# Opening of a cross-attention block: the query weights split by column groups, four token blocks turned in a row, small vectors on another queue

## The reference, cut to what matters

```python
x = x + _L0_xattn_ref(_layernorm(x, axis=-1), ctx_1024, ctx_1024, mask, W_q, b_q, W_k, b_k, W_v, b_v, W_o, b_o)

def _L0_xattn_ref(q, k, v, mask, ...):
    Q = split_heads(q @ W_q + b_q)      # 16 heads of 32
    K = split_heads(k @ W_k + b_k)
    V = split_heads(v @ W_v + b_v)
    scores = jnp.einsum('bhqd,bhkd->bhqk', Q, K) / math.sqrt(D_K)
    ...
```

## Time and profile before

| what | us |
|---|---|
| median of three runs | 741.67 |
| the profiled execution | 741.27 |
| its span, first to last instruction | 739.5 |
| PE busy | 709.2 |
| DVE busy | 406.5 |
| ACT busy | 326.5 |
| POOL busy | 202.7 |

### The profile page before, as it was taken

How to read it: one execution, slowest core, us unless ns; L and a number is a source line. 1 busy time by engine, 2 the same in 40 slices (tenths; PEclk the granted TensorE clock), 3 DMA queues, 4 the chain that set the end, 5 groups by cost and what they waited for, 6 DMA issues and landing times.

```text
span 739.5 us, 18487 instructions
## 1 busy us (share of the span) xinstructions
PE 709.2 (96%) x7369; PEld 575.9 (78%) x7384; DVE 406.5 (55%) x1089; ACT 326.5 (44%) x700; POOL 202.7 (27%) x160
## 2 busy tenths in 40 slices
PE   4999999999999999999999999999998999999976
PEld 1788888888888888888888888877776767766743
DVE  4833323323665345345343323349478888887886
ACT  3425456455344344344344344455224524433434
POOL 2610001000987647647530000001122122113110
PEclk9999999999999999999999999999999999999999
DMA  7242333332132231231121121626001011101201
GB/s 256 93 175 61 120 122 107 128 121 89 36 122 84 89 118 35 89 117 36 32 64 32 32 64 33 228 60 242 1 1 30 1 42 43 43 1 43 43 1 44
DMA packets 46632, 56.83 MB, mean 77 GB/s; under 512 B 15088, under 2 KB 35824, under 8 KB 45328
## 3 DMA queue, kind: packets, MB, share of 16 engines
q1 hardware_dynamic: 41840, 39.20, 17.3%
q0 software_dynamic: 3328, 16.78, 6.4%
q10 hardware_dynamic: 1440, 0.53, 0.3%
HBM read 51.19 MB, written 2.16 MB: 72 GB/s over the span
## 4 chain that ended last, share of the span: by engine, by line
PE 82%; DVE 10%; issue 4%; DMA 2%; ACT 1%; SPq 0%; DVEq 0%; POOL 0%; ACTq 0%
PE bank L231 66%; PE bank L437 4%; PE bank L595 3%; PE bank L451 3%; PE bank L428 3%; DVE s_sb L1388 2%; DMA stage<-in_w_xq 2%; PE bank L558 1%; DMA stage<-in_w_xo 1%; DVE X L1446 1%; DVE y_quant L1354 1%; DVE h_max L1395 1%; DVE h_sb L1372 0%; DVE y_sb L1363 0%; PE bank L459 0%
## 5 line engine op out<-in xcount | busy, mean ns | idle before, releaser
L231 PE MATMUL bank<-ctx_high,wk_high 128*128 128x258 f32 x512 | 147.4, 288 | 0.1
L231 PE MATMUL bank<-ctx_low,wk_high 128*128 128x258 f32 x512 | 144.6, 282 | 0.0
L231 PE MATMUL bank<-ctx_high,wk_low 128*128 128x258 f32 x512 | 144.1, 282 | 0.0
L231 PEld LDWEIGHTS bank<-ctx_high,wk_high 128*128 128x128 f32 x512 | 96.8, 189 | 13.7 <-issue 13.4
L231 PE MATMUL bank<-wv_high,ctx_high 128*128 128x512 f32 x256 | 105.9, 414 | 0.0
L791 ACT ACTIVATE vals<-bank 128x512 f32<-128x512 f32 x64 | 38.3, 598 | 144.2 <-PE bank L231 144.2
L231 PE MATMUL bank<-wv_low,ctx_high 128*128 128x512 f32 x256 | 101.2, 395 | 0.0
L231 PE MATMUL bank<-wv_high,ctx_low 128*128 128x512 f32 x256 | 100.9, 394 | 0.0
L231 PEld LDWEIGHTS bank<-ctx_low,wk_high 128*128 128x128 f32 x512 | 96.7, 189 | 0.0
L231 PEld LDWEIGHTS bank<-ctx_high,wk_low 128*128 128x128 f32 x512 | 96.5, 188 | 0.0
L781 ACT ACTIVATE kT<-bank,bxk 128x257 f32<-128x257 f32 x128 | 60.3, 473 | 56.5 <-PE bank L231 56.3
(11 more groups left out here) (217 smaller groups left out, 1359.0 us busy)
## 6 DMA issues: line engine op xcount, KB each, us to landing
raw<-in_ctx_t SPq DMA_DIRECT2D x32, 514.0 KB, 4.0
stage<-in_w POOLq DMA_DIRECT2D x16, 1024.0 KB, 5.9
X<-in_x SPq DMA_DIRECT2D x4, 512.0 KB, 4.2
v_last<-last_values SPq DMA_DIRECT2D x32, 64.0 KB
out<-X SPq DMA_DIRECT2D x8, 256.0 KB, 2.3
stage<-in_w_xv SPq DMA_DIRECT2D x1, 1024.0 KB, 8.1
stage<-in_w_xq SPq DMA_DIRECT2D x1, 1024.0 KB, 11.5
stage<-in_w_xk SPq DMA_DIRECT2D x1, 1024.0 KB, 5.7
```

The lines of the kernel that those rows point to most:

```text
L231: last = pe.matmul(to, left(i, c), right(j, c), start=(c == 0 and i + j == 0), stop=(c == C - 1 and i == 1))
```

## The change

- The query weights are split in four groups of 128 output columns, each over all four chunks: ACT makes the four high parts one after the other, DVE the four low parts. POOL's part in it is gone. Each of the first four query products waits for its own group (`wxq_low`, and `weights_low` for the fourth).
- Token blocks use three PSUM banks (0, 1, 2) instead of two, so `turn_x(t)` waits for `x_low(t - 3)`. `xn` still has two buffers.
- ACT copies all four first blocks before it touches the query weights. DVE measures blocks 2 and 3 before it scales block 0, and finishes the four `x_low` before the four low parts of the weights.
- PE turns blocks 2 and 3 after `project_last(0)` and does `project_last(1..3)` behind them; blocks 4 and 5 are turned after queries 1 (before: after queries 0), 6 and 7 after queries 2 (before: after queries 1). ACT follows: `keep_queries(0)`, `keep_queries(1)`, blocks 4 and 5, `keep_queries(2)`, blocks 6 and 7, W_v.
- The eight small transfers are issued by SP behind W_q instead of by ACT.

```diff
 # SP
             load_weight(1)
             load_weight(0)
+            for dst, src in small:
+                sp.dma_start(dst, src).then_inc(small_landed, 16)
             staged_ready(sp, 0)
 # PE
-                if t >= 2:
-                    pe.wait_ge(xT_low, t - 1)
+                if t >= 3:
+                    pe.wait_ge(xT_low, t - 2)
...
+                if half == 0:
+                    pe.wait_ge(*((wxq_low, g + 1) if g < C - 1 else (weights_low, 1)))
...
             project_last(0)
             turn_x(2)
-            project_last(1)
             turn_x(3)
-            project_last(2)
-            project_last(3)
-            pe.wait_ge(weights_low, 1)
-            pe.wait_ge(wxq_rest_low, 1)
-            for k in range(2):
-                project_queries(k)
-                turn_x(4 + 2 * k)
-                turn_x(5 + 2 * k)
+            for c in range(1, C):
+                project_last(c)
+            project_queries(0)
+            project_queries(1)
+            turn_x(4)
+            turn_x(5)
             project_queries(2)
+            turn_x(6)
+            turn_x(7)
 # ACT
-            for dst, src in small:
-                act.dma_start(dst, src).then_inc(small_landed, 16)
...
-            x_high(0)
-            x_high(1)
+            for t in range(C):
+                x_high(t)
             staged_ready(act, 0)
-            act.activation(wxq[0][:, 2:4, :], stage[0][:, 2:4, :], ACT.Copy).then_inc(wxq_rest_high, 1)
-            x_high(2)
-            act.activation(wxq[0][:, 0:2, :], stage[0][:, 0:2, :], ACT.Copy).then_inc(weights_high, 1)
-            x_high(3)
+            for g in range(C):
+                part = slice(g * P, (g + 1) * P)
+                act.activation(wxq[0][:, :, part], stage[0][:, :, part], ACT.Copy).then_inc(
+                    wxq_high if g < C - 1 else weights_high, 1)
...
-            for k in range(2):
-                keep_queries(k)
-                x_high(4 + 2 * k)
-                x_high(5 + 2 * k)
+            keep_queries(0)
+            keep_queries(1)
+            x_high(4)
+            x_high(5)
+            keep_queries(2)
+            x_high(6)
+            x_high(7)
             split_weight(1)
-            keep_queries(2)
             keep_queries(3)
 # POOL
-                if k == 2:
-                    pool.wait_ge(wxq_rest_high, 1)
-                    pool.tensor_tensor(wxq[1][:, 2:4, :], stage[0][:, 2:4, :], wxq[0][:, 2:4, :].bitcast(F32),
-                                       ALU.subtract).then_inc(wxq_rest_low, 1)
 # DVE
             measure_x(0)
+            measure_x(1)
             scale_x(0)
-            measure_x(1)
             scale_x(1)
+            scale_x(2)
             x_low(0)
-            scale_x(2)
-            x_low(1)
             scale_x(3)
-            x_low(2)
-            dve.wait_ge(weights_high, 1)
-            dve.tensor_tensor(wxq[1][:, 0:2, :], stage[0][:, 0:2, :], wxq[0][:, 0:2, :].bitcast(F32),
-                              ALU.subtract).then_inc(weights_low, 1)
-            x_low(3)
+            for t in range(1, C):
+                x_low(t)
+            for g in range(C):
+                part = slice(g * P, (g + 1) * P)
+                dve.wait_ge(*((wxq_high, g + 1) if g < C - 1 else (weights_high, 1)))
+                dve.tensor_tensor(wxq[1][:, :, part], stage[0][:, :, part], wxq[0][:, :, part].bitcast(F32),
+                                  ALU.subtract).then_inc(wxq_low if g < C - 1 else weights_low, 1)
```

More of the change, by code:

```diff
@@ L168, in build_block @@
         weights_high, weights_low = sem("weights_high"), sem("weights_low")
-        lastT_landed, wxq_rest_high, wxq_rest_low = sem("lastT_landed"), sem("wxq_rest_high"), sem("wxq_rest_low")
+        lastT_landed, wxq_high, wxq_low = sem("lastT_landed"), sem("wxq_high"), sem("wxq_low")
         placed_landed = {"v": sem("v_landed"), "g": sem("g_landed")}
@@ L270, in load_weight @@
                     sp.wait_ge(weights_low, n - 1)
-                    if n == 2:
-                        sp.wait_ge(wxq_rest_low, 1)
                     if n == 3:
@@ L356, in turn_x @@
                 pe.wait_ge(x_scaled, t + 1)
-                if t >= 2:
-                    pe.wait_ge(xT_low, t - 1)
+                if t >= 3:
+                    pe.wait_ge(xT_low, t - 2)
                 for c in range(C):
-                    last = pe.transpose(bank[t % 2][:, c * P:(c + 1) * P], xn[:, t % 2, c * P:(c + 1) * P], idf[:, :])
+                    last = pe.transpose(bank[t % 3][:, c * P:(c + 1) * P], xn[:, t % 2, c * P:(c + 1) * P], idf[:, :])
                 last.then_inc(x_turned, 1)
@@ L741, in x_high @@
                 act.wait_ge(x_turned, t + 1)
-                act.activation(xT[t // C][0][:, :, t % C * P:(t % C + 1) * P], bank[t % 2][:, :].rearrange("p (c n) -> p c n", c=C),
+                act.activation(xT[t // C][0][:, :, t % C * P:(t % C + 1) * P], bank[t % 3][:, :].rearrange("p (c n) -> p c n", c=C),
                                ACT.Copy).then_inc(xT_high, 1)
@@ L1153, in x_low @@
                 high, low = [part[:, :, t % C * P:(t % C + 1) * P] for part in xT[t // C]]
-                dve.tensor_tensor(low, bank[t % 2][:, :].rearrange("p (c n) -> p c n", c=C),
+                dve.tensor_tensor(low, bank[t % 3][:, :].rearrange("p (c n) -> p c n", c=C),
                                   high.bitcast(F32), ALU.subtract).then_inc(xT_low, 1)
```

## The result

Nine runs of the changed kernel gave a median of 739.59 us (738.44 to 741.62), nine of the kernel before beside them 742.32 us (741.31 to 743.54). The ratio is 0.9967, with a 95% interval of 0.9956 to 0.9978: by the ratio 2.45 us faster, and between 1.6 and 3.3 (the two medians alone differ by 2.73). The prediction was 740.0 us with a gain of 1.65 us, "same within 0.3%" at 0.67. The time lies in the range of 738.6 to 741.6; the gain is larger than forecast and on the far side of the 0.3% line, though its interval reaches back over it. The profiled execution lasted 739.59 us, and 739.6 was forecast for it.

What follows compares the result with a forecast made beforehand. TensorE's opening, up to the first key matmul, was taken to decide: 2.05 us gained at the queries less 0.4 given back makes 1.65, so 741.27 falls to 739.6, or 740.0 us on the median's footing; range 738.6 to 741.6.

Steps and rivals of the forecast that it cites:

- The bound: Loop from 43.60 to 464 us: TensorE works without a hole, so any opening shift passes undiminished to the end.
- K: Start of the first key matmul, ending the opening; 43.60 us before, forecast near 42.0.
- TensorE up to the queries: Opening: first transposes move from 8.28 to 8.75 us, then work without gaps; queries forecast to start at 17.1.
- S: Start of the first query matmul; 19.15 us before, forecast 17.1.
- the clock's share: Opening: the clock's rise puts the query start between 16.4 (splits then limit it) and 18.0; gains 2.3 to 0.7 us.
- the forecast's first condition: Opening: TensorE's clock rises 4.4 us after unbroken work begins, near 13.2 us.
- Weights and small vectors: Opening: weight splits don't decide the query start, and moving eight small transfers to SP has price 0.
- From S to the keys: First query to first key matmul: 24.9 us, with about 1.2 us waiting for the context behind POOL's addition.
- The term that was mis-sized: Gain at the start of the queries: forecast 2.05 us, of which 0.4 is given back before the keys.
- A: At the keys: context not late, TensorE alone decides; keys at 40.8, gain 2.8 us, 738.9 us; chance 0.17.
- B: Opening: small vectors hold SP, x blocks 4 to 7 issued 3.7 us later; gain 1.0, 740.7 us; chance 0.08.
- C: Opening: TensorE stays at 1.2 GHz, keys at 45.2; 1.6 us later, 743.3 us; chance 0.06.

Runs made afterwards that it cites:

- Experiment 5: Changed kernel with twenty unread identity transposes on TensorE ahead of block 0; 738.10 us, ratio 0.9940 to the kernel before.
- experiment 1: Changed kernel with GpSimd's bias addition put behind the second context split; 738.15 us, ratio 0.9937 to the kernel before.
- experiment 3: Changed kernel with blocks 4 and 5 turned after queries 0, 6 and 7 after queries 1; 741.91 us, ratio 0.9983 to the kernel before.
- experiment 6: Changed kernel with both the twenty early transposes and GpSimd's addition behind the second context split; 736.05 us, ratio 0.9923 to the kernel before.
- experiment 4: Changed kernel with the eight small transfers issued by ACT again; 739.48 us, ratio 0.9961 to the kernel before.
- Experiment 10: Changed kernel with project_last(1) between the turns of blocks 2 and 3; 740.11 us, ratio 0.9965 to the kernel before.
- experiment 2: Kernel before with GpSimd's bias addition put behind the second context split; 742.77 us, ratio 1.0002.
- again: Kernel before, unchanged, profiled once more in one execution; 743.38 us.
- experiment 9: Kernel before with ten identity transposes behind project_last(3), filling the gap before the queries; 741.92 us, ratio 1.0001.
- experiment 7: Kernel before with twenty identity transposes on TensorE ahead of block 0; 743.06 us, ratio 1.0007.
- experiment 8: Kernel before with only the low part of W_q's chunks 2 and 3 moved from GpSimd to VectorE; 741.98 us, ratio 0.9987.

## Why the prediction was right, and where it was off

**The bound.** From 43.60 us on a shift passes to the end: held. Time less K is the same in both kernels' first profiles, 697.67 and 697.60; what moves it is the clock at the end, in both kernels.

**TensorE up to the queries.** First transposes at 8.75 forecast, 8.74 measured; S at 17.1, measured 17.21 and 17.28, TensorE without a hole. Experiment 5 shows that the clock's rise is the term, as the paragraph on the clock's share said: with it out of the way S is 15.2. That 17.1 was so near is partly luck, for two errors cancel. Eight transposes in a row took 1.87 us to the next start at the low level (8.74 to 10.61), not twice the 1.05 of the forecast, which makes S earlier by about 0.4. The rise came later than either moment that the forecast weighed, 13.2 and 14.5: worked out from the starts of the rows, the durations halve near 14.7 and 14.8 in the two profiles of the changed kernel. The same program up to the queries ran in four profiles (changed twice, 1, 3): S was 17.21, 17.28, 16.59 and 16.02. The Trainium skill's page "TensorE: Matmul & The Clock Gate", section "Part 1: The HAM clock gate", has the moment of the rise differ from run to run; these four agree, with 1.26 us between them. TensorE began at 8.74 to 8.78 in all four, so the rise did not follow the beginning of its work at one distance, as the forecast's first condition had it: worked out as above it came near 13.3 in experiment 1 and 12.1 in experiment 3. The forecast's lower end for S, 16.4, was a little too high, and the reason given for it, that the splits would take over there, did not hold: in experiments 3, 5 and 6 the queries start at 16.02, 15.18 and 14.69 without a wait for them.

**Weights and small vectors.** Price 0 for both; experiment 4 gives nothing to 0.36 us. Experiment 10 shows that in the other order the splits do become the bound, by 0.27 us. The third bank was not tried by itself; the profile of the changed kernel bears out its price of nothing, since x_low(0) and x_low(1) end at 11.18 and 12.23, before the turn of block 2 starts at 12.46, so that two banks would have been free as well.

**From S to the keys.** S + 24.9 forecast, S + 24.78 measured; the wait 1.2 forecast, 0.89 shown as idle (1.07 by experiment 1). That GpSimd's addition holds VectorE, and that it decides only after the change, is shown by experiments 1 and 2 together. The Trainium skill's page "SBUF — State Buffer", section "SBUF: two separate sides", with its lock held for the whole instruction agrees: 7.61 us with the addition beside it, 2.29 without.

**The term that was mis-sized** is the difference of the two S. The forecast took 19.15 less 17.1 = 2.05 us, with the 19.15 from one profile of before. That execution had W_q at 13.79; in the three other profiles where the kernel before has its order (again, 2 and 9) it landed at 14.2, and S was 19.53 to 19.56. The mean of the four is 19.45. For the changed kernel the mean of its four is 16.78. That makes 2.67 at S, less the 0.33 given back between S and K: 2.34 us, beside the measured 2.45 (1.6 to 3.3). Both single profiles stood at the end of their spread that makes the gain small: the page of before was an early one, the page of after a late one. They agree with the forecast so well partly for that reason.

**The rivals.** A (no wait for the context) is excluded by the 0.89 us. B (SP held by the small vectors) is excluded: SP issued x blocks 4 to 7 at 12.95, earlier than the 13.81 of before. Its sum has a slip: 13.81 and 3.7 make 17.5 and not 17.2, and its gain about 0.8 instead of 1.0. C (low clock throughout) didn't occur in the changed kernel, but the mechanism is real where a gap is left, as experiments 3 and 7 show.

**Not settled**: why W_q lands at 13.8 in one profile of the kernel before and at 14.2 in three; what decides whether the clock falls at the end of an execution, four times in fourteen behind the same gap; whether the kernel before sometimes loses it ahead of its queries too (experiment 9); and what VectorE's new order of measuring is worth by itself.

## What to carry to other kernels

When an edit pulls a bound forward, write down the next thing as "S plus so much" and take both sums, with and without the cover: here they were 1.2 us apart by the forecast and 1.07 by the runs, and each was met to about 0.1. An instruction that was free in the old order (GpSimd's addition) can hold the new one; look for long instructions that begin in the opening and ask who stands behind them. And size a term that varies from run to run from several executions, or give it as a spread: one profile of each kernel understated this gain by a third.

## What the runs showed of the hardware that was not expected

- An idle stretch of TensorE can cost more than itself: after 1.93 us of idle time the granted clock went to its lower level and the next product's matmuls started 0.43 us apart instead of 0.23 (experiment 3); after 3.71 us likewise (experiment 7). Gaps of 0.79 to 1.52 us ahead of the queries did not lose it in five profiles of the kernel before and its variants (both profiles, 2, 8 and 9), but behind the 1.51 us near the end it was lost in four profiles of fourteen.
- Extra work can be a gain: twenty transposes whose result nobody reads made the changed kernel's keys start 2.05 us earlier (39.94 against 41.99).
- The granted clock column reads 1.00 from 5 to 14 us, although the same transposes and `project_last` take nearly twice as long there as later. In the first microseconds the durations say it, not that column.
- Where the small transfers were issued by ACT, W_q landed at 13.8 to 14.3 us; behind W_q on SP's queue, at 12.8 to 13.4.
